# Transposes in pairs, sums for three tile groups, and a rebuilt last stage in a state-space, convolution and FFN kernel on one Trainium2 core

## The reference, cut to what matters

```
a   = per-sequence 32x32 mix of x (weights from a small MLP and softmax) + bias
p   = a @ in_proj.T                     # gate 4096 | x 4096, B 1024, C 1024 | dt 64
xBC = silu(causal 4-tap convolution of p[x,B,C])
dt  = softplus(p[dt] + dt_bias);  dA = exp(-exp(A_log) * dt)
state = state*dA + (dt*x) outer B;  y = state . C + D*x        # scan over 32 steps, 64 heads
yn  = y * rsqrt(mean over 512 of y*y + 1e-5) * norm_weight * silu(gate)    # in 8 groups
x   = x + yn @ out_proj.T
z   = grouped 9-tap convolution of x over the features + context
out = x + mask(z) * (z @ W.T + b)       # mask from softmax(z @ centroids.T / 0.1) > 0.01
```

## Time and profile before

| | |
|---|---|
| median of 3 runs | 1662.33 us (1658.47 to 1663.17) |
| the profiled execution | 1662.89 us, its span 1661.1 us |
| TensorE busy | 1619.4 us, 97% of the span; mean granted clock 0.991 |
| DVE, ACT, POOL busy | 64%, 52%, 47% |
| stages | seg of stage 0 at 67.6 us, of stage 31 at 1508.0 us |

### The profile page before, as it was taken

One profiled execution on the slowest core, in us unless ns is written; L12 is line 12 of the kernel. 1 busy time (PEld: TensorE's weight loads), 2 busy tenths in 40 slices (PEclk: granted clock), 3 DMA queues, 4 the chain that ended last, 5 costly groups with the idle time before them and its releaser, 6 DMA issues.

```text
span 1661.1 us, 31702 instructions
## 1 busy us (share of the span) xinstructions
PE 1619.4 (97%) x12495; PEld 1300.1 (78%) x12495; DVE 1066.9 (64%) x1772; ACT 857.0 (52%) x1378; POOL 780.9 (47%) x766
## 2 busy tenths in 40 slices
PE   9999999999999999999999999999999999998997
PEld 6678888888888888877778888888888888886665
DVE  6967666566656566777676656665656666564456
ACT  4654546555555555455554555555555545554221
POOL 4464645545463636444254554546364645544103
PEclk9999999999999999999999999999999999999999
DMA  6110102011111111020112201111011102016772
GB/s 202 35 58 29 43 20 64 27 52 39 46 45 33 58 34 43 16 64 26 33 39 71 65 27 52 39 41 50 33 58 33 39 20 65 27 35 148 167 164 102
DMA packets 50291, 93.09 MB, mean 56 GB/s; under 512 B 5664, under 2 KB 6304, under 8 KB 50144
## 3 DMA queue, kind: packets, MB, share of 16 engines
q1 hardware_dynamic: 50144, 91.06, 19.0%
HBM read 82.59 MB, written 8.45 MB: 55 GB/s over the span
## 4 chain that ended last, share of the span: by engine, by line
PE 81%; issue 7%; ACT 4%; POOL 4%; DVE 3%; POOLq 0%; DVEq 0%
PE PS L478 47%; PE PS L744 19%; PE PS L592 3%; PE PS L1084 2%; PE PS L1030 2%; PE PS L650 2%; PE PS L711 2%; ACT big L533 1%; PE PS L357 1%; PE PS L602 1%; PE PS L570 1%; DVE cb L513 1%; POOL yl L704 1%; PE PS L571 1%; PE PS L206 1%
## 5 line engine op out<-in xcount | busy, mean ns | idle before, releaser
L478 PE MATMUL PS<-xh,wh 128*128 128x512 f32 x1280 | 529.7, 414 | 0.6 <-DVE xl L367 0.6
L478 PE MATMUL PS<-xh,wl 128*128 128x512 f32 x1280 | 503.2, 393 | 0.0
L478 PE MATMUL PS<-xl,wh 128*128 128x512 f32 x1280 | 500.3, 391 | 0.0
L513 DVE SCALAR_TENSOR_TENSOR cb<-PS,P,cb 128x496 f32<-128x496 f32 (+2 forms) x576 | 412.6, 716 | 98.4 <-ACT cb L499 82.7
L182 POOL TENSOR_TENSOR wl<-rw,wh 128x512 fp32r<-128x512 f32 x160 | 207.4, 1299 | 183.6 <-ACT wh L177 165.2
L478 PEld LDWEIGHTS PS<-xh,wl 128*128 128x128 f32 x1280 | 240.5, 188 | 55.9
L478 PEld LDWEIGHTS PS<-xh,wh 128*128 128x128 f32 x1280 | 241.1, 188 | 46.2 <-ACT wh L177 1.0
L478 PEld LDWEIGHTS PS<-xl,wh 128*128 128x128 f32 x1280 | 241.9, 189 | 43.1
L698 POOL TENSOR_TENSOR ysum<-yq 128x256 f32<-128x256 f32 x128 | 95.5, 746 | 375.4 <-ACT yq L686 375.4
L499 ACT ACTIVATE cb<-PS,P 128x512 f32<-128x512 f32 x192 | 149.2, 777 | 221.2 <-PE PS L478 220.9
L744 PE MATMUL PS<-oh,yh 128*128 128x512 f32 x512 | 203.0, 396 | 6.4 <-POOL yl L704 5.4
(11 more groups left out here) (193 smaller groups left out, 2238.1 us busy)
## 6 DMA issues: line engine op xcount, KB each, us to landing
rw<-in_w_in SPq DMA_DIRECT2D x160, 256.0 KB, 2.7
ro<-in_w_out SPq DMA_DIRECT2D x64, 256.0 KB, 2.9
wh<-x2s SPq DMA_DIRECT2D x32, 258.5 KB, 5.0
wl<-x2s SPq DMA_DIRECT2D x32, 258.5 KB, 5.2
x2s<-acc SPq DMA_DIRECT2D x16, 260.0 KB, 4.0
out_x<-acc SPq DMA_DIRECT2D x16, 256.0 KB, 2.3
acc<-in_x SPq DMA_DIRECT2D x3, 1024.0 KB, 9.6
acc<-in_x SPq DMA_DIRECT2D x4, 256.0 KB, 4.1
```

What stands on the lines that cost most here:

```text
L478: fn = lambda e, k=k, w=w, v=v, i=i: e.matmul(PS[:, bank, :], w[:, m, 128 * k:128 * k + 128], v[:, k, a:a + 512], start=(i == 0), stop=(i ...
L513: dve.op(lambda e, d=d, w=w: e.scalar_tensor_tensor(out=cv[:, :, d:32], in0=pv[:, :, 0:32 - d], scalar=w, in1=cv[:, :, d:32], op0=ALU.mult ...
```

## The change

It has these parts.

1. `A` puts tiles 0 and 1 in slot 7 and tiles 2 and 3 in slot 9, through the banks 2, 5, 2, 7. `A_dve` of both tiles of a pair stands in slot 8 and in slot 0, ahead of `M_dve` of both in slot 9 and slot 1.
2. `S` multiplies with one column of ones instead of 128, and is called for tile 0 (slot 1), tiles 1 and 2 together (slot 4) and tile 3 (slot 5), after their O; `rstd` follows per group, three times instead of four, and `acc` of tile 1 moves from slot 4 to slot 5.
3. The 33rd stage is replaced by `last_products`, with another order of the same work: the convolution of tile 0 ahead of O of tile 0, that of tile 1 behind O of tile 1, S for two tiles at a time, all O ahead of the first `turn`. The FFN weight splits come behind the y chain, two low parts on POOL and two on DVE, and the fourth piece has a buffer of its own.

The diff, cut to its core (unindented shifts of `if real:` left out):

```diff
-        yss = sb("yss", [128, 2, 128])
+        yss = big[:, 7168:7680].rearrange("p (i t) -> p i t", i=4)
+        TB = (PT, PO[2], PT, PO[0])
+        def sums(n):
+            return ((0,), (1, 2), (3,)) if n < NS - 1 else ((0, 1), (2, 3))
...
         def A(n, i):
+            if i == 0:
+                for m in range(6):
+                    pe.wait("silu", (n, m))
+                if n >= 1:
+                    pe.wait("dtx", (n - 1, 2))
...
+            elif i == 1:
+                pe.wait(*(("acc", (n - 1, 2)) if n >= 1 else ("xl", 7)))
+            elif i == 2:
+                pe.wait("dtx", (n, 0))
+            else:
+                pe.wait("L", (n, 0))
...
+                fn = lambda e, j=j: e.transpose(PS[:, TB[i], 128 * j:128 * j + 128], xs[:, j, a:a + 128], ident)
...
+        def S(n, tiles):
+            last = (n, tiles[-1])
+            pe.wait("ys2", last)
+            pe.wait(*shared[0])
+            shared[0] = ("var", last)
+            for i in tiles:
+                fn = lambda e, i=i: e.matmul(PS[:, PG, 256 + i:257 + i], yss[:, i, :], C[:, C_ONE:C_ONE + 1], start=True, stop=True)
...
+        def rstd(n, tiles):
+            a, b, last = tiles[0], tiles[-1] + 1, (n, tiles[-1])
+            dve.wait("S", last)
...
+            dve.op(lambda e: e.tensor_scalar(vr[:, a:b], PS[:, PG, 256 + a:256 + b], 1.0 / 512.0, 1e-5, ALU.mult, ALU.add), "var", last)
+            pool.wait("var", last)
...
         def O(n, i):
             if i == 0:
-                pe.wait("L", (n, 0))
+                pe.wait("dtx", (n, 3))
...
-                    when = dict(O=(1, 3, 4, 5), rstd=(2, 4, 5, 6), acc=(2, 4, 5, 6)) if real else ...
+                    when = dict(O=(1, 3, 4, 5), acc=(2, 5, 5, 6))
...
+                    if m == 0:
+                        A_dve(n - 1, 2)
+                        A_dve(n - 1, 3)
+                    if m == 1:
+                        M_dve(n - 1, 2)
+                        M_dve(n - 1, 3)
...
+                if m == 7:
+                    seg(n)
+                    expo(n)
+                    A(n, 0)
+                    A(n, 1)
+                if m == 9:
+                    A(n, 2)
+                    A(n, 3)
+                    Y(n, 0)
+                    Y(n, 1)
...
-        sp.wait("fl", 0)
+        sp.wait("silu", (end_n, 5))
         sp.op(lambda e: e.dma_start(raws[3], w_ffn[3]), "ld_f3", 0, 16)
...
-            pool.wait("fh", k)
+            eng = pool if k < 2 else dve
+            eng.wait("fh", k)
...
+        def last_products():
+            n = end_n
+            conv2(0)
+            load_G(4)
+            y_dve(n, 0)
+            y_act(n, 0)
+            y_pool(n, 0)
+            x3_act(0)
+            A_dve(n, 2)
+            A_dve(n, 3)
+            M_dve(n, 2)
+            M_dve(n, 3)
+            for i in (1, 2, 3):
+                y_dve(n, i)
+                y_act(n, i)
+                y_pool(n, i)
+            for k in range(4):
+                weights2(k)
+            O(n, 0)
+            Y(n, 2)
+            Y(n, 3)
+            O(n, 1)
+            S(n, (0, 1))
+            conv2(1)
+            load_G(5)
+            x3_act(1)
+            O(n, 2)
+            O(n, 3)
+            S(n, (2, 3))
+            for tiles in sums(n):
+                rstd(n, tiles)
+                for i in tiles:
+                    add_out(n, i)
+
+        for n in range(NS):
             stage(n)
-        for step in range(5, NT + 2):
+        last_products()
+        for step in range(1, NT + 2):
+            if step == 1:
+                one_hot()
             second(step)
```

More of the change, by code:

```diff
@@ L455, in adaln_attn_ffn_kernel, with summed @@
         shared = [("mx", 3)]
+        def sums(n):
+            return ((0,), (1, 2), (3,)) if n < NS - 1 else ((0, 1), (2, 3))
+        def summed(n, i):
+            return next(g[-1] for g in sums(n) if i in g)
         def who(n):
@@ L642, in Y @@
                 pe.wait("L", (n, 1))
+                pe.wait("dtx", (n, 1))
                 if n >= 1:
@@ L709, in S @@
             pe.wait(*shared[0])
[L710 to L720, removed]
@@ L722, in rstd_pool @@
-        def rstd_pool(n, i):
-            z = 4 * n + i
-            pool.wait("var", (n, i))
-            pool.wait("mh", 0)
-            if z >= 4:
-                pool.wait("acc", divmod(z - 4, 4))
-            pool.op(lambda e: e.tensor_tensor(rs[:, i:i + 1], vr[:, i:i + 1], mh[:, 0:1], ALU.pow), "rs", (n, i))
+            shared[0] = ("var", last)
+            for i in tiles:
+                fn = lambda e, i=i: e.matmul(PS[:, PG, 256 + i:257 + i], yss[:, i, :], C[:, C_ONE:C_ONE + 1], start=True, stop=True)
+                pe.op(fn, "S", last) if i == tiles[-1] else pe.op(fn)
@@ L807, in stage @@
                 chain.extend(D_chain(0))
-            for m in range(10 if real else 7):
+            for m in range(10):
                 lag = 1
@@ L818, in stage @@
                 if prev:
-                    when = dict(O=(1, 3, 4, 5), rstd=(2, 4, 5, 6), acc=(2, 4, 5, 6)) if real else dict(O=(1, 2, 3, 4), rstd=(2, 3, 4, 5),
-                                                                                                   acc=(2, 3, 4, 5))
+                    when = dict(O=(1, 3, 4, 5), acc=(2, 5, 5, 6))
                     at = lambda kind: [i for i in range(4) if when[kind][i] == m]
-                    for i in at("rstd"):
-                        rstd_dve(n - 1, i)
-                        rstd_pool(n - 1, i)
+                    for tiles in sums(n - 1):
+                        if when["acc"][tiles[-1]] == m:
+                            rstd(n - 1, tiles)
                     for i in {0: (0,), 1: (1,), 3: (2, 3)}.get(m, ()):
-                        if i == 2 and real:
+                        if i == 2:
                             G_mask(n)
@@ L895, in stage @@
                         Y(n - 1, 3)
[L896 removed]
+                if m == 2:
                     G_all(n)
@@ L902, in stage @@
                         O(n - 1, i)
[L903 to L921 removed]
+                        for tiles in sums(n - 1):
+                            if tiles[-1] == i:
+                                S(n - 1, tiles)
+                if m == 7:
[3 more added lines that the diff above has]
+                    A(n, 1)
+                if m == 9:
+                    A(n, 2)
+                    A(n, 3)
+                    Y(n, 0)
+                    Y(n, 1)
         end_n = NS - 1
@@ L1071, in ffn @@
             pe.wait("x3l", T)
-            pe.wait("fl", 3)
+            pe.wait("fl0", 1)
+            pe.wait("fl1", 1)
             if c == 0 and T >= LATE + 4:
```

143 lines of the change are left out of this document (57 added, 86 removed).

## The result

The changed kernel takes 1652.37 us, median of 6 runs (1650.19 to 1654.88), where the kernel before took 1662.39 beside it: a ratio of 0.9942, 95% interval 0.9927 to 0.9957. The prediction was 1650, range 1641 to 1657, faster with 0.90. The number held. Of its three large terms one was right, one had the right size although two statements behind it were wrong, and one was three times too small.

A forecast was written before the change was run, and what follows sets the result against it. TensorE, busy 97% of the span, was taken as the bound. Pairs -4.5, late add +1.9 and last stage -9.1 sum to -11.7: from 1662.9 to 1651.2, as a median 1650.6, stated as 1650; range 1641 to 1657.

The forecast's parts named there:

- TensorE as the bound: Whole kernel: TensorE is busy 97% of the span, so what it issues and where it idles sets the time.
- the other engines are far from that: Ordinary stage: engines other than TensorE are far from its 45.47 us from seg to seg.
- The narrow sums: Sums with one column of ones for 128 stay two weight loads of 0.11: no gain, ends 0 and 27.
- The pairs: Transposes of two tiles together save changeovers of 0.05 between projections: 0.15 in each stage, 4.5 us over 30.
- The new waits cost nothing in an ordinary stage: Ordinary stage: tile 3's transposes have over 3 us to spare, O of tile 0 has 1.6 of slack, less 0.5.
- One power less on POOL and one small operation less on DVE lie beside a busy TensorE and bring nothing: Ordinary stage: the work saved on POOL and DVE was priced at no gain.
- The late add: Tile 1's add, one slot later, delays dt transposes in stages 1 and 17: 1.8 late, net 0.95, together +1.9.
- The last stage: 33rd stage, reordered: Y to first ffn 26.4 against 36.99; -10.8 with the second ffn's wait, -9.1 with one clock fall.
- A: Rival: narrow sums free the weight loads, 0.1 to 0.22 per sum, 12 to 27 us more, 1623 to 1638; 8%.
- B: Rival: the last stage gives little, its waits and clock falls stay, and the pairs bring nothing: 1656 to 1661; 9%.
- C: Rival: the clock falls in ordinary stages, 1.65 lost in each, 51 us over 31 stages, about 1702; 4%.
- D: Rival: the change does not do what it says, the fill and pairs only moving waits: 1660 to 1665; 4%.

The follow-up runs named there:

- both: The changed kernel with tile 1 summed separately behind dt blocks only, and on POOL tile 3's power between the two decay products: 1646.39 us, ratio 0.9914.
- The loop made shorter: The changed kernel with one sum per tile again outside the last stage, and on POOL tile 3's power between the decay products: 1651.12 us, ratio 0.9946.

## Why the prediction held, and where its steps did not

**TensorE as the bound** was right for the kernel before, but "the other engines are far from that" was wrong as an argument. DVE and POOL are busy 64% and 47%, and still the loop through them ended 0.2 to 0.6 ahead of seg, where 0.1 is the least. A share of busy time can't show that.

**The narrow sums**, forecast at 0 with ends 0 and 27: measured 0.07 a stage, 2 us, inside the interval of no change. The weight loads were the right row. The Trainium skill's "TensorE: Matmul & The Clock Gate", section "Back-to-back issue gap", gives the figure behind the prediction's 21 us (an estimate) for an isolated matmul, and says itself that in a stream of weight loads and matmuls both set the spacing. A sum here is such a pair, twice over, and the ratio 0.9993 agrees with that. The section "LDWEIGHTS (loading the stationary operand)" of the same page of the Trainium skill has a load's time set by the columns of the weights; the loads 0.11 apart agree.

**The pairs**, forecast at 0.15 a stage: the sum came out at 0.17, and "45.3 instead of 45.47" at 45.28. The reason holds for TensorE's own part: where the loop is out of the way, in the kernel "both", the stage is 45.20, against 45.38 with one column alone. What failed is the account of the other engines. The step that failed is "The new waits cost nothing in an ordinary stage", with its companion "One power less on POOL and one small operation less on DVE lie beside a busy TensorE and bring nothing". The first looked only at whether tile 3's transposes could start in time, and not at Y, which they push back; pairs alone cost 0.31 a stage. The second called worthless the very edit that pays for this: with pairs, merging is worth 45.77 - 45.28 = 0.49. The prediction did say that 0.5 of excess "would eat the whole gain", and sought it at O, where there was slack, and not at seg, where there was none. It was luck that two errors cancelled.

**The late add**, forecast at +1.9 in all: +3.0 and +2.6. The place, the cause and the bounds (to +10) were right; the term was mis-sized threefold. Times of two executions can be compared here only when counted from seg of stage 16, which stands at 823.88 before and at 825.11 in the changed kernel:

```profile
823.88 0.39 PE L570 MATMUL PS<-yh,uf 128*128 128x512 f32 x1
825.11 0.39 PE L578 MATMUL PS<-yh,uf 128*128 128x512 f32 x1
```

So counted, DVE reached the variance at 38.28 instead of 39.18, the 0.9 earlier that was forecast, and the first add ended at 40.07 (forecast 39.92; a power of two columns takes 0.16 longer than one of one). The dt transposes began at 40.21 instead of 37.89, 2.3 late where the forecast's times give 2.0 and it counted 1.8, and the idle 0.86 at seg went as forecast. What the sum left out, and named only as an end, is the fall of the clock behind the wait: apart from that idle time, the stretch from the dt transposes to seg takes 1.2 more than before (875.57 - 865.32 = 10.25, for 871.71 - 861.77 - 0.86 = 9.08). Late start and slow clock less the idle time make the 2.6. That the wait is 3.2 long and not 1.8 has another cause: TensorE was there at 37.00, where 38.09 was forecast, largely since in the kernel before it waits 0.19 and 0.27 for dtx in this stage (at 831.54 and 836.54) and with the pairs it does not. Some of the single DVE operations differ by up to 1 us between the two traces (one dt operation took 1.46 for 0.41, another 0.51 for 1.36); why is open.

**The last stage**, forecast at -9.1: measured -9.5 (-8.9 from seg of stage 31 to the first ffn, which holds the moved transposes, and -0.5 behind it, where the second ffn's wait of 0.59 is gone). From Y to first ffn it is 27.68; the forecast was 26.4 and one fall of the clock. Wait by wait: 1.83 behind the first convolution (forecast 1.6), 0.34 at the second O ("just in time"), 1.89 for DVE (forecast 1.3). The clock fall of 1.65 did not come, and the longer waits took its place. That it did not was in part luck: the kernel of "The loop made shorter" has the same order and the same wait (1.82), and there the clock fell. The removal runs confirm the terms: the fill's 2.78 are hidden whole, the DVE parts give 1.4, and the order as a whole 8.8.

**The rivals.** A fell with one column alone. B fell with the old last stage. C, falls of the clock in ordinary stages, did not come: 45.20 to 45.57 in the 26 of them. D fell with the same run as B. What came close to turning the sign was no rival at all: pairs without the merge are slower than before, 1.0050.

## What to carry to other kernels

Before an edit inside a loop of stages is priced by the bound engine's own time, follow the loop that crosses stages back through the other engines, and measure how far ahead of the bound engine's next wait it ends; a stage that shows no wait can be 0.2 us from one. Operations that only move ahead of another on the bound engine delay what the others get from it, so price both sides. And where several edits share a stage, undo them one at a time and in pairs before any one is credited: here the merge was worth 0.02 or 0.49, depending on the other edit.

## What the runs showed of the hardware beyond that

The low parts of the FFN weights took 1.45 to 1.46 each on POOL with DVE idle beside it. When both worked, the first on POOL, with DVE beside it from its first 0.4 us on, took 1.45, the second 1.94, and those on DVE 1.64 and 1.97, so the split over two engines ended in 3.95 us (1534.75 to 1538.70) instead of 5.61 (1533.14 to 1538.75), not in half. A power on POOL takes 0.55 for one column and 0.71 for two. The granted clock fell to 0.50 behind a wait of 1.63 at a sum in a stage's middle, and stayed at 1.00 through the last stage, whose waits were 1.83, 0.34 and 1.89 (windows of the changed kernel):

```profile
1518.00:1545.40 27.40, 23.34 (x261) 14.53 (x253) 17.20 (x24) 9.85 (x16) 15.21 (x16) 1.00 0.89 212
```

In the kernel of "The loop made shorter", whose last stage has the same order, the granted clock fell to 0.50 behind the same wait of 1.82 for yl, and its last stage is 1.5 longer:

```profile
1518.30:1521.60 3.30, 3.30 (x25) 2.17 (x27) 0.38 (x1) 0.94 (x2) 2.42 (x3) 0.50 1.04 322
```

So the length of a wait alone did not decide whether the clock fell.
